# One more wait on GpSimd: each chunk's four gathers of the second graph layer are waited for before the next chunk's are issued

## The reference

```python
proj = feat @ fc_weight.T
el = proj[src]
er = proj[dst]
e = jnp.sum(jax.nn.leaky_relu(el + er, NEG_SLOPE) * a, axis=-1)
gate = jax.nn.sigmoid(jnp.sum(el * er, axis=-1))
w = jax.nn.sigmoid(e * gate)
msg = feat[src] * w[:, None]
neigh_sum = jax.ops.segment_sum(msg, dst, num_segments=N)
neigh = neigh_sum / jnp.maximum(deg, 1.0)[:, None]
rst = (1.0 + eps[0]) * feat + neigh
```

## Time and profile before

| | |
|---|---|
| time of the kernel before | 4246.06 us, median of 3 runs (4229.13 to 4255.51) |
| span of the profiled execution, first to last instruction | 4202.4 us |
| time of the profiled execution itself | not listed apart from its span |
| busy in the span | PE 2278.9 us, DVE 2546.9, ACT 1628.2, POOL 2103.2 |
| gathers of layer 2 | 1624 (406 chunks of 4), 950 ns each |

### The profile page before, as it was taken

How to read it: one execution, slowest core, us unless ns; L and a number is a source line. 1 busy time by engine, 2 the same in 40 slices (tenths; PEclk the granted TensorE clock), 3 DMA queues, 4 the chain that set the end, 5 groups by cost and what they waited for, 6 DMA issues and landing times. The chain is left out here.

```text
span 4202.4 us, 64915 instructions
## 1 busy us (share of the span) xinstructions
PE 2278.9 (54%) x13842; PEld 1815.0 (43%) x13842; DVE 2546.9 (61%) x12793; ACT 1628.2 (39%) x3531; POOL 2103.2 (50%) x2223
## 2 busy tenths in 40 slices
PE   1757575756667783445544444454444444444444
PEld 1535353544445443444443443444444444444443
DVE  6535353534444275667666676666676767667667
ACT  2424242433333244444443443443444444434344
POOL 3252434343343203666656565666656666656652
PEclk9878787878878896666666666656666666656666
DMA  7121111111111215444444444444444445444443
GB/s 145 32 54 31 51 34 48 38 44 42 41 48 34 58 49 169 138 132 136 134 133 129 123 137 128 130 137 128 136 125 131 134 132 139 129 135 129 128 129 96
DMA packets 357885, 425.07 MB, mean 101 GB/s; under 512 B 174163, under 2 KB 242141, under 8 KB 357740
## 3 DMA queue, kind: packets, MB, share of 16 engines
q0 software_dynamic: 103728, 266.13, 22.4%
q1 hardware_dynamic: 251800, 156.64, 14.5%
q10 hardware_dynamic: 2212, 0.60, 0.1%
HBM read 399.44 MB, written 23.70 MB: 101 GB/s over the span
## 5 line engine op out<-in xcount | busy, mean ns | idle before, releaser
L1449 POOL DMA_INDIRECT got<-rows,idx x1624 | 1543.0, 950 | 1038.3 <-issue 487.4
L1618 PE MATMUL sum_ps<-whot,got 128*128 128x128 f32 x3264 | 762.0, 410 | 1146.7 <-remote 416.6
L1618 PEld LDWEIGHTS sum_ps<-whot,got 128*128 128x128 f32 x3264 | 660.8, 301 | 1236.9 <-remote 433.6
L763 POOL DMA_INDIRECT got<-x_rows,idx x532 | 516.5, 971 | 789.5 <-DMA idx<-src_rows 630.7
L918 ACT CAST work<-c_ps 128x318 bf16<-128x318 f32 x1092 | 451.3, 431 | 845.0 <-remote 439.6
L945 PE MATMUL span_ps<-x_parts,work 128*126 128x393 bf16 x2756 | 667.9, 353 | 20.0 <-issue 20.0
L1611 PE MATMUL er_ps<-win,hot_t 128*128 128x128 bf16 x4932 | 525.4, 284 | 204.4 <-issue 121.0
L994 PE MATMUL c_ps<-right,left 128*128 128x318 bf16 x1092 | 338.0, 317 | 467.9 <-issue 281.2
L1611 PEld LDWEIGHTS er_ps<-win,hot_t 128*128 128x128 bf16 x4932 | 476.9, 134 | 234.7 <-issue 131.6
L1461 DVE TENSOR_SCALAR whot<-iota_f,dl,w_s 128x128 f32<-128x128 f32 x1632 | 477.5, 359 | 124.1 <-issue 121.7
L1517 DVE CUSTOM_DVE_ANT_0 small_rows<-got,er_ps 128x128 f32<-128x128 f32 x1624 | 387.3, 281 | 154.6 <-issue 116.3
(11 more groups left out here) (240 smaller groups left out, 2101.7 us busy)
## 6 DMA issues: line engine op xcount, KB each, us to landing
work<-dst_row SPq DMA_DIRECT2D x413, 256.0 KB
got<-rows,idx POOLq DMA_INDIRECT x1624
win<-parts SPq DMA_DIRECT2D x118, 96.0 KB
got<-x_rows,idx POOLq DMA_INDIRECT x532
idx<-src_rows SPq DMA_DIRECT2D x413, 2.0 KB
parts<-split SPq DMA_DIRECT2D x13, 384.0 KB
x_rows<-x_parts SPq DMA_DIRECT2D x2, 2320.5 KB
rows<-nodes SPq DMA_DIRECT2D x13, 256.0 KB, 2.8
```

The source lines that it names most:

```text
L763: pool.indirect_dma_start(got[:, c, i, 0:3 * D], None, x_rows, bass.IndirectOffsetOnAxis(ap=idx[:, c, i:i + 1], axis=0)).then_inc(gathered ...
L1449: pool.indirect_dma_start(got[:, c, i, :], None, rows, bass.IndirectOffsetOnAxis(ap=idx1[:, c, i:i + 1], axis=0)).then_inc(gathered[c], 16)
L1618: mm = pe.matmul(sum_ps[:, 0:P], got[:, c, i, D:2 * D], whot[:, c, i, :], start=(c == 0 and i == 0), stop=(c == NS - 1 and i == STEP - 1))
```

## The change

One line is added to POOL's program of layer 2. After the four gathers of chunk c POOL waits until all four have landed (each adds 16 to `gathered[c]`), before it goes on to the next chunk's waits and gathers. DVE's and SP's waits on the same semaphore are as before.

```diff
@@ -1450,6 +1450,7 @@
                                     got[:, c, i, :], None, rows,
                                     bass.IndirectOffsetOnAxis(ap=idx1[:, c, i:i + 1], axis=0)
                                 ).then_inc(gathered[c], 16)
+                            pool.wait_ge(gathered[c], 16 * STEP * k + 16 * STEP)
 
                 @block.vector
                 def _(dve):
```

## The result

The changed kernel takes 4840.4 us (4825.4 to 4846.8, 4 runs) beside 4239.0 us of the kernel before on the same chip: **1.140 times as long** (95% interval 1.137 to 1.144). The forecast was 4815 us, the range 4602 to 4950.

A forecast was written before the change was run, and what follows sets the result against it. Layer 2 ran at 6.23 us per chunk, POOL held by the ring; POOL's new chain, 3.80 + 3.1 + 0.77 = 7.67 us, over 400 steps adds 576 us, less 4 at the end: forecast 4815 us, range 4602 to 4950.

The forecast's parts named there:

- The bound: Layer 2: no engine is full; the ring holds POOL and consumers hold the ring, at 6.23 us per chunk.
- The first term: POOL, layer 2: first to fourth gather of a chunk, three intervals of 1.267 us, 3.80 us, as before.
- The landing: Layer 2: from the fourth gather's start until a waiting engine knows it has landed, 3.1 us per chunk.
- SP's loads "at no cost": Layer 2: SP's row load after the landing serves a match two chunks later, 15 us, so adds nothing.
- The time itself: Whole kernel: predicted span 4774 us plus 43.7 us between profiled span and median gives 4818, stated as 4815 us.
- The wake-up: POOL: from a landing to its next gather, 0.77 us per chunk, taken from an index load in layer 1.
- No cost at the start, -4 us at the end: Layer 2: filling five chunks hides in POOL's 23.27 us idle; DVE's last distance shrinks from 7.24 to about 3.1 us.
- POOL's old waits go away: Layer 2: POOL's long waits for PE's sums and "remote", 527.3 us, vanish and do not come on top.
- Rival (b): Layer 2: the ring still stops POOL for half of 1.32 us per chunk; period 8.33 us, 5082 us; chance 0.09.
- Rival (a): Layer 2: the landing is cheaper than SP shows, 7.13 us per chunk, 4602 us; chance 0.18.
- Rival (c): Layer 2: no slower, or faster if spaced gathers let DVE run, 6.0 us per chunk, 4154 us; chance 0.03.
- The estimate of 2.30 us: Layer 2 landing from about 2.0 us fixed plus bytes; period 6.87 us, result 4498 us; not used in the sum.

The follow-up runs named there:

- the slightly cheaper variant: The changed kernel with POOL's waits for the next chunk's indices and ring slot moved ahead of the landing wait: 4238.4 us beside 3213.6, ratio 1.319.

## Why the prediction was right

**The bound.** It took the pace from first and last chunk, 6.23 us, saw POOL held by the ring and by delays of its consumers, and put a new floor beside it. The larger of the two paces was the right form: three waits of seven changed nothing, since their floor was 6.22; waits for the previous chunk changed nothing; a wait for every chunk gave the floor itself.

**The first term** (3.80 us for four gathers to be issued): 3.85 measured. The mean duration went from 950 to 953 ns and the usual gap stayed 0.30.

**The landing** (3.1 us as SP sees it, 3.87 with the wake-up): 3.91 us measured on average from fourth gather to next gather. That it fits so well is partly luck, because two errors cancel. The usual landing was taken too long, since it is 3.72 us with the wake-up and 2.91 as SP sees it in the row above. And two costs were left out: 1.0 us behind the second chunk of each body, where the prediction had SP's loads "at no cost", and 0.3 us where the loop turns, together 0.19 us a chunk. The period was 0.09 us short of the measured 7.76, half from this term and half from the first: 35 us in 400 chunks, of the 49 us by which the 620.8 us between the profiled spans exceed +572. The other 14 us are the later start.

**The time itself** missed by 25 us and not by 49, and that is luck too. The prediction added the 43.7 us by which the median of the runs lay above the profiled span; for the changed kernel that distance is 4840.4 - 4823.2 = 17.2 us. It says only which of the runs was profiled.

**The wake-up** (0.77 us, from layer 1): 0.83 us later than DVE. SP's load and POOL's next gather lie 0.77 us apart in the row above. From POOL's last semaphore event to the gather it is 0.75 us behind every landing. A row of another stage with another wait gave it well.

**No cost at the start, -4 us at the end**: the end came out so (3.19 us). Chunk 5 began 14 us later, though, after a first gather that came 19 us later (1620.18 against 1600.87): POOL's last gather of layer 1 came 17 us later in that execution (1423.99 against 1406.93), and the fill itself made 5 us of it good.

**POOL's old waits go away**: 527.3 to 4.6 us. Rival (b), that they remain in part, is refuted by that row, and the run with three waits of seven shows the replacement.

**Rival (a)**, the cheap landing from the gap of 3.33 us, fell: that gap ended with a signal from PE and not with a landing, and the waits for a landing in the changed kernel's rows above have 2.73 to 3.87 us of idle time, where that gap had 2.38.

**Rival (c)** had a true half. DVE's delays do go with dense gathers (what makes them is open, see the last section), and in the changed kernel they are gone from layer 2: DVE's idle time of 118.9 us before `whot` is 6.1 us. But as it said itself, POOL's chain is a floor above 6.23 whatever DVE does. No run here tests the sharing of ports that it names beside this.

The estimate of 2.30 us for such a gather, from the page "DMA: Bandwidth & Descriptors" of the Trainium skill, section "Anatomy of one DMA — SWDGE (gpsimd) path", was too low here. The medians of the changed kernel are 2.41 us from a gather's start to its last packet and 2.89 until DVE starts.

## What to carry to other kernels

A wait costs what it exposes, less the waits that it replaces: compute the floor of the waiting engine's own chain (issue, landing, wake-up) and set it against the present pace; only what lies above counts, and if the present pace comes from something that may vanish, the same wait costs far more. A landing's price for an engine that never waited for it can be read from one that did. If a wait is needed at all, wait for the chunk before the one just issued: that was free here, in a kernel whose waiting engine had 1.32 us a chunk to spare. Whether it is free without that room was not measured; two gathers earlier it was not (4.3% slower). And look at each place in the loop's body by itself: the late landings sit in the same chunks every time, and an average hides them.

## What the runs showed of the hardware that was not expected

The same kernel on the same chip took 4223 us beside two series and 3214 us beside one. Where it takes 4223, engines wait long for signals with no recorded sender ("remote") in both layers (in layer 1, from 200 to 1400 us, ACT alone 409.3 us before L918), and DVE stands still between instructions; the profiles of the second series have next to none of either. With one gather per chunk, and in the changed kernel, where DVE works mostly between two landings, this is gone from layer 2 in the same series; in layer 1, which these edits don't touch, it is not (398.7 and 410.3 us before L918). With half the bytes it stays (4265 us). The changed kernel has as many gathers as the kernel before, so it goes with how densely they come, and not with their number or their data.

"Remote" has to be read with care here, because the traces are incomplete just where it appears. Of the two counts that POOL makes per chunk on the semaphore `chunk_begun`, 812 in layer 2, the trace of the kernel before holds 450 and that of the changed kernel all 812. The half-bytes kernel left 23,191 semaphore events in the third series and 66,780 in the second, with the same program. A "remote" wait may thus be a wait for a sender whose event is missing. Whether the engines are delayed by something in the chip, or by the recording of so many events itself, no run here tells apart: that rival is untested. Nor is it known why one series was free of it. The price of the change hangs on it: 14% where the delays are, and 32% for the slightly cheaper variant where they are not.
